# Forming only the first layer's first shift and scale before the first part, and the other modulations at its end

## The reference, cut to what matters

```
mod = (silu(L0_c) @ L0_wmod).reshape(16, 6, 1, 256)   # L0_c 16x256, L0_wmod 256x1536
sa, ca, ga, sb, cb, gb = mod[:, 0..5]
ga = (2 * (ga >= 0) - 1) * maximum(abs(ga), 0.25)     # gb alike
h  = layernorm(x) * (1 + ca) + sa
x  = x + ga * attn0(h, Wq, Wk, Wv, Wlr, Wg, Wo, ...)  # projections, short convolution over 4 taps, SiLU,
                                                      # unit length per head, a recurrence over 32 chunks of 16 tokens
h  = layernorm(x) * (1 + cb) + sb
x  = x + gb * ffn0(h, U1, V1, b1, U2, V2, b2)
# layer 1 the same with L1_c, L1_wmod: windowed attention, then a gated feed-forward part
```

## Time and profile before

| quantity | value |
|---|---|
| median of three runs | 2527.85 us (2524.26 to 2531.57) |
| profiled execution, its own time | 2533.14 us |
| its span | 2531.3 us |
| TensorE (PE) matmul busy | 2166.9 us, 86% |
| VectorE (DVE) busy | 1596.6 us, 63% |
| ScalarE (ACT) busy | 1576.2 us, 62% |
| GpSimd (POOL) busy | 1086.6 us, 43% |
| setup, to the first projection | 0 to 55.5 us |
| part A and its end | 55.5 to 452.4 us |
| mean granted TensorE clock | 0.933 of 2.4 GHz |

### The profile page before, as it was taken

The page is one execution under the profiler, slowest core; times in us unless marked ns, Lnnn a source line. Parts: engine busy times, 40 slices in busy tenths (PEclk is TensorE's granted clock), DMA queues, the critical chain, the costliest instruction groups (busy, mean ns, idle before and its releaser), DMA issues.

```text
span 2531.3 us, 88431 instructions
## 1 busy us (share of the span) xinstructions
PE 2166.9 (86%) x32563; PEld 1390.6 (55%) x32563; DVE 1596.6 (63%) x3896; ACT 1576.2 (62%) x4079; POOL 1086.6 (43%) x1204
## 2 busy tenths in 40 slices
PE   5999997487788787787389999999999999999898
PEld 4554454255555555455246566575664756647466
DVE  1888886477666666667247477474764747647465
ACT  2788787377676666667248466484654846547464
POOL 0122122377677677667524423344233442334323
PEclk8999999699788888889699999999999999999999
DMA  4455555623233233231421231312213122130120
GB/s 150 126 158 164 162 156 160 119 68 85 66 79 74 68 85 76 56 72 39 137 52 31 71 75 43 94 32 66 67 48 94 42 58 60 52 89 4 39 50 18
DMA packets 403135, 201.57 MB, mean 80 GB/s; under 512 B 273776, under 2 KB 389104, under 8 KB 402688
## 3 DMA queue, kind: packets, MB, share of 16 engines
q1 hardware_dynamic: 402688, 195.65, 29.6%
HBM read 101.67 MB, written 69.27 MB: 68 GB/s over the span
## 4 chain that ended last, share of the span: by engine, by line
PE 55%; ACT 15%; issue 12%; DVE 12%; POOL 3%; DMA 1%; SPq 1%; ACTq 0%; DVEq 0%; POOLq 0%
PE psum L982 11%; PE psum L763 6%; ACT arena L1492 6%; ACT arena L1292 5%; PE psum L1075 4%; DVE arena L1785 4%; PE psum L834 3%; PE psum L846 3%; PE psum L1034 3%; PE psum L841 3%; PE psum L1042 3%; PE psum L1111 3%; PE psum L1148 2%; PE psum L1098 2%; PE psum L1129 2%
## 5 line engine op out<-in xcount | busy, mean ns | idle before, releaser
L1716 POOL TENSOR_TENSOR arena<-arena 128x400 f32<-128x400 f32 x256 | 218.3, 853 | 482.8 <-DVE arena L2132 482.8
L1292 ACT ACTIVATE arena<-psum,scan_sb 64x128 f32<-64x128 f32 x1152 | 308.3, 361 | 106.0 <-PE psum L911 88.4
L1492 ACT ACTIVATE arena<-psum,arena 128x100 f32<-128x100 f32 x1024 | 269.5, 365 | 6.0 <-DVE arena L2124 5.9
L1785 DVE SCALAR_TENSOR_TENSOR arena<-psum,taps_sb,arena 128x511 f32<-128x511 f32 (+2 forms) x288 | 213.8, 747 | 60.7 <-ACT arena L1201 53.9
L1534 POOL TENSOR_TENSOR arena<-arena 128x512 f32<-128x512 f32 x64 | 79.4, 1274 | 359.0 <-ACT arena L1227 359.0
L763 PE MATMUL psum<-arena,w_in_sb 128*128 128x512 f32 x512 | 230.0, 598 | 0.9 <-issue 0.9
L841 PE MATMUL psum<-arena 128*32 128x17 f32 x10240 | 134.9, 191 | 98.3 <-issue 65.1
L1852 DVE TENSOR_TENSOR arena<-psum,scan_sb 64x512 f32<-64x512 f32 x290 | 189.0, 673 | 7.6 <-PE psum L942 7.6
L846 PE MATMUL psum<-arena,scan_sb 128*128 128x512 f32 x264 | 186.5, 799 | 1.9 <-DVE arena L1852 1.9
L841 PEld LDWEIGHTS psum<-arena 128*32 128x32 f32 x10240 | 115.5, 117 | 123.1 <-issue 71.7
L2124 DVE TENSOR_REDUCE arena<-psum 128x4 f32<-128x400 f32 x256 | 146.4, 573 | 57.1 <-PE psum L1098 46.7
(11 more groups left out here) (220 smaller groups left out, 4712.2 us busy)
## 6 DMA issues: line engine op xcount, KB each, us to landing
arena<-arena SPq DMA_DIRECT2D x144, 128.0 KB
arena<-x SPq DMA_DIRECT2D x32, 512.0 KB, 3.9
arena<-gates_d SPq DMA_DIRECT2D x112, 128.0 KB, 4.0
v_rows_d<-arena SPq DMA_DIRECT2D x64, 136.0 KB
k_rows_d<-arena SPq DMA_DIRECT2D x64, 136.0 KB
arena<-k_rows_d SPq DMA_DIRECT2D x128, 68.0 KB, 2.0
arena<-v_rows_d SPq DMA_DIRECT2D x128, 68.0 KB, 2.2
v_d<-arena SPq DMA_DIRECT2D x32, 256.0 KB, 4.3
```

The costliest lines, as they stand in the source:

```text
L1292: ins = act.activation(dst.rearrange("p (t x a) -> p t x a", x=PP, a=INNER)[upper, :, x], src.rearrange("p (t a) -> p t a", a=INNER)[upper ...
L1492: act.activation(c_soft[s][:, f % 2, u], sc, ACT.Exp, bias=c_max[s][:, u:u + 1]).then_inc(c_act.mark(f"exp{s}{f}u{u}"), 1)
L1716: pool.tensor_tensor(soft, soft, c_rec[s].unsqueeze(2).broadcast_to([P, 4, KEYS]), ALU.mult).then_inc(c_pool.mark(f"prob{s}{f}"), 1)
L1785: ins = dve.scalar_tensor_tensor(out=a_acc[:, t, j:TOK], in0=bank[2 + t][:, 0:TOK - j], scalar=taps_sb[:, t % KT, col:col + 1], in1=a_acc[ ...
```

## The change

The modulations are now all formed as rows (`mod_row(c)`: 16x512, two of the twelve rows of 256 at once, c = 0 for layer 0's first shift and scale, c = 1 to 5 for the others), and those that are needed as columns are turned afterwards (`mod_turn`, a transpose of a 16x128 piece to 128x16).

Before part A only c = 0 is formed, copied by ScalarE (`row0`), turned with 4 transposes (`mod0`), copied (`modc0`) and its scale raised by 1 (`plus1`). At the end of part A TensorE forms c = 1 to 5 between `turn_v` and `turn_k` of the last sequence, VectorE copies each out of PSUM, forms the gates, copies the 20 turned pieces (`mod1`), adds 1 to the other three scales and makes the bfloat16 identity.

The loads are reordered: `cond`, the first third of layer 0's `wmod` (512 KB), the identity and `parity`, x of sequence 0, `taps`, `w_in`, `mean16`; after x of sequence 1 the rest of `wmod` and the other 22 weights. The waits on all 24 weights become waits on the single ones. `phase_a_done` waits for `identb` and the 22 weights in place of the store of the gates; the last is waited for on SP ahead of the first load of gates in part C.

```diff
-            for layer in range(LAYERS):
-                sp.dma_start(wmod_sb[:, layer], wmod[layer].rearrange("(k p) n -> p k n", p=P)).then_inc(wmod_loaded, 16)
-            for dst, src in ((ident[:], ident_c), (mean16[:], blocks_c), (parity[:], parity_c)):
+            sp.dma_start(wmod_sb[:, 0, :, 0:2 * DIM], wmod[0, :, 0:2 * DIM].rearrange("(k p) n -> p k n", p=P)).then_inc(wmod_first, 16)
+            for dst, src in ((ident[:], ident_c), (parity[:], parity_c)):
                 sp.dma_start(dst, src).then_inc(consts_loaded, 16)
-            for dst, src in (
-                (w_in_sb[:], w_in.rearrange("(k p) n -> p k n", p=P)),
...
-            sp.wait_ge(su_pe.sem, su_pe.before(1, "gate1"))
-            sp.wait_ge(su_dve.sem, su_dve.before(1, "gates"))
-            sp.dma_start(gates_d[0:BATCH], gates_row).then_inc(gates_stored, 16)
...
             load_x(0)
+            sp.dma_start(taps_sb[:], taps.rearrange("(k p) n -> p k n", p=P)).then_inc(taps_loaded, 16)
+            sp.dma_start(w_in_sb[:], w_in.rearrange("(k p) n -> p k n", p=P)).then_inc(w_in_loaded, 16)
+            sp.dma_start(mean16[:], blocks_c).then_inc(blocks_loaded, 16)
             next_x(1)
+            sp.dma_start(wmod_sb[:, 0, :, 2 * DIM:], wmod[0, :, 2 * DIM:].rearrange("(k p) n -> p k n", p=P)).then_inc(wmod_loaded, 16)
+            sp.dma_start(wmod_sb[:, 1], wmod[1].rearrange("(k p) n -> p k n", p=P)).then_inc(wmod_loaded, 16)
+            load_weights()
             next_x(2)
...
+            sp.wait_ge(su_dve.sem, su_dve.at(0, "gates"))
+            sp.dma_start(gates_d[0:BATCH], gates_row).then_inc(gates_stored, 16)
...
+            def mod_row(c):
+                layer, third = THIRDS[c]
+                for k in range(KT):
+                    mm = pe.matmul(bank[max(c + 1, 2)][0:BATCH], cond_silu[:, layer, k], wmod_sb[:, layer, k, third * 2 * DIM:(third + 1) * 2 * DIM],
+                                   start=(k == 0), stop=(k == KT - 1))
+                mm.then_inc(su_pe.mark(f"row{c}"), 1)
...
             pe.wait_ge(su_act.sem, su_act.at(0, "silu"))
+            pe.wait_ge(wmod_first, 16)
+            mod_row(0)
+            pe.wait_ge(consts_loaded, 32)
+            pe.wait_ge(su_act.sem, su_act.at(0, "row0"))
+            mod_turn("mod0", 0, first_rows, 0, 2 * KT)
...
             turn_v(BATCH - 1)
+            pe.wait_ge(wmod_loaded, 16 * LAYERS)
+            pe.wait_ge(pr_act.sem, pr_act.at(BATCH - 1, "g1"))
+            for c in range(1, 6):
+                if c == 3:
+                    pe.wait_ge(le_act.sem, le_act.at(BATCH - 1, "ln3"))
+                mod_row(c)
             turn_k(BATCH - 1)
+            pe.wait_ge(su_dve.sem, su_dve.at(0, "row5"))
+            mod_turn("mod1", 7, other_rows, 2 * KT, LAYERS * N_MOD * KT)
...
-            act.wait_ge(su_dve.sem, su_dve.at(0, "gates"))
+            act.wait_ge(su_dve.sem, su_dve.at(0, "tap"))
+            act.wait_ge(su_dve.sem, su_dve.at(0, "plus1"))
...
+            for c in range(1, 6):
+                dve.wait_ge(su_pe.sem, su_pe.at(0, f"row{c}"))
+                dve.tensor_copy(other_rows[:, (c - 1) * 2 * DIM:c * 2 * DIM], bank[c + 1][0:BATCH]).then_inc(su_dve.mark(f"row{c}"), 1)
+            dve.wait_ge(pr_act.sem, pr_act.at(BATCH - 1, "silu5"))
+            gate_rows_made()
+            dve.wait_ge(su_pe.sem, su_pe.at(0, "mod1"))
+            dve.tensor_copy(modc[:, 2 * KT:].rearrange("p a b -> p (a b)"), bank[7][:, 0:(LAYERS * N_MOD - 2) * KT * BATCH]).then_inc(su_dve.mark("modc1"), 1)
+            dve.wait_ge(su_dve.sem, su_dve.at(0, "modc1"))
+            for j, which in ((2, 4), (3, 7), (4, 10)):
+                add_one(f"plus{j}", which)
+            dve.tensor_copy(identb[:], ident[:]).then_inc(su_dve.mark("identb"), 1)
```

More of the change, by code:

```diff
@@ L140, in adaln_two_layers @@
         cond_silu = carve(LAYERS, KT, BATCH)
[L141 to L144, removed]
+        first_rows = carve(2 * DIM)[0:BATCH]
+        gates_row = carve(2 * LAYERS * DIM)[0:BATCH]
+        THIRDS = [(layer, third) for layer in range(LAYERS) for third in range(N_MOD // 2)]
         top[0] = 0
@@ L711, in _, with mod_turn @@
                 pe.sem_inc(st.sem, len(st.names))
-            pe.wait_ge(wmod_loaded, 16 * LAYERS)
-            pe.wait_ge(su_act.sem, su_act.at(0, "silu"))
[L715 to L728, removed]
+            def mod_row(c):
[4 more added lines that the diff above has]
+                mm.then_inc(su_pe.mark(f"row{c}"), 1)
+            def mod_turn(name, b, rows, first, last):
+                for m in range(first, last):
+                    mm = pe.transpose(bank[b][:, (m - first) * BATCH:(m - first + 1) * BATCH], rows[:, (m - first) * P:(m - first + 1) * P], ident[0:BATCH, 0:BATCH])
+                mm.then_inc(su_pe.mark(name), 1)
+            pe.wait_ge(su_act.sem, su_act.at(0, "silu"))
+            pe.wait_ge(wmod_first, 16)
[3 more added lines that the diff above has]
+            mod_turn("mod0", 0, first_rows, 0, 2 * KT)
             def turn(m):
@@ L752, in project @@
                     elif name in ("q0", "q1"):
[L753 removed]
+                        if behind:
+                            pe.wait_ge(pr_act.sem, pr_act.before(n, ("g0", "g1")[j]))
                     elif behind:
@@ L1169, in _ @@
             act.activation(cond_silu, cond_sb, ACT.Silu).then_inc(su_act.mark("silu"), 1)
[L1170 to L1174, removed]
+            act.wait_ge(su_pe.sem, su_pe.at(0, "row0"))
+            act.activation(first_rows, bank[2][0:BATCH], ACT.Copy).then_inc(su_act.mark("row0"), 1)
+            act.wait_ge(su_pe.sem, su_pe.at(0, "mod0"))
+            act.activation(modc[:, 0:2 * KT].rearrange("p a b -> p (a b)"), bank[0][:, 0:2 * KT * BATCH], ACT.Copy).then_inc(su_act.mark("modc0"), 1)
             def norm_a(m):
@@ L1737, in _ @@
                 dve.sem_inc(st.sem, len(st.names))
[L1738 to L1744, removed]
-            dve.wait_ge(weights_loaded, 16 * 24)
@@ L1752, in _, with add_one @@
[L1752 to L1756 removed]
+            def add_one(name, which):
+                cols = modc[:, which * KT:(which + 1) * KT]
+                dve.tensor_scalar(cols, cols, 1.0, None, ALU.add).then_inc(su_dve.mark(name), 1)
```

105 lines of the change are left out of this document (60 added, 45 removed).

## The result

The changed kernel takes 2552.28 us (median of 4 runs, 2551.34 to 2554.3), the kernel before beside it 2526.06 us (4 runs, 2519.92 to 2531.57). The ratio is 1.009, with a 95% interval of 1.0062 to 1.0118: slower by 26 us (0.9%), where 36.5 us less were forecast, with a range of 2484.5 to 2499. The profiled execution took 2551.96 us, its span 2550.2.

A forecast was written before the change was run, and what follows sets the result against it. Setup before part A was taken as serial, with TensorE idle 9.08 us at part A's end to take the moved work. 37.0 - 0.5 - 0 = 36.5 us off 2527.85 gives 2491.3, range 2484.5 to 2499.

The forecast's parts named there:

- The head: Before part A: first transposes start at 15.7 us where they stood at 52.67, a gain of 37.0, ends 33.9 and 39.
- x of sequence 2: Load in part A, issued half a microsecond late behind the moved weights: 0.5 us of loss counted, ends 0 and 5.
- The end of part A: Five rows fill TensorE's hole before `turn_k` in 8.6 us at the fast clock: no cost, ends 0 and 8.6.
- The rivals on transfers and on slow rows: Early transfers bind: gain 28 to 33.5, chance 0.15; rows slow at part A's end: 7.4 us lost, chance 0.08.
- Part B, the step that failed: Part B's clock wanders from slice to slice, untied to the work; no new mean, noise of 4 us either way.
- turning point: In part B: the change comes out slower once a chunk takes 1.4 us more in the mean.
- part B loses the clock, and the kernel is slower: Rival: engines enter part B from another state; 2 us more a chunk gives 2555; chance 0.03, 0.02 of it ending slower.
- what would show the prediction wrong: First projection after 24 us, row passes at part A's end taking 0.86, or part B over 20 us longer or shorter.

The follow-up runs named there:

- 128 more: The changed kernel with 128 empty semaphore increments added to TensorE's program at the end of part A: 2494.88 us against 2535.31 for the kernel before, ratio 0.9823.
- 64 more: The changed kernel with 64 empty semaphore increments added to TensorE's program at the end of part A: ratio 1.0002 to the kernel before.
- 192 more: The changed kernel with 192 empty semaphore increments added to TensorE's program at the end of part A: ratio 0.9948 to the kernel before.

## Why the prediction was wrong, point by point

- **The head, 37.0 us forecast:** 36.96 came (52.67 - 15.71). The first product started at 5.38 (5.2 forecast), row 0 took 3.57 (3.4, the slow pace), the transposes of the modulations 0.57 (1.0), the copy of 128x64 0.22 (0.3), the first projection stood at 18.61 (18.5).
- **x of sequence 2, a loss of 0.5:** issued at 34.07, it let VectorE start at 41.87, 7.8 us later, where x of sequence 0 alone had taken 3.69 before; so it did stand behind the weights. VectorE had waited 1.96 us for it, and ScalarE took up that layer norm at 43.82, which is no later than the shifted time (81.41 - 36.96 = 44.45). The loss is nothing.
- **The end of part A, no cost:** rows at the fast pace took 8.76 (8.6), `turn_k` waited for POOL, the twenty transposes took 1.41 (2.6 to 5), `identb` was made from 409.30 to 409.52, 5.5 us ahead of SP's 414.98. Right, with more room than was reckoned.
- **The rivals on transfers and on slow rows:** neither came.
- **Part B, the step that failed.** The prediction called the pattern of the granted clock and of the long chunks "not tied to the work" and wrote: "three runs lie within 7.3 us, so the wandering averages out; I see no reason for a new mean". The pattern of the long chunks is tied to the program; it comes back every 8 chunks at the same instructions, with stops at the joints of 16 KB pieces of code. Runs of one program can't show this, since all of them have the same grid; their narrow spread says only that the mean of this program is steady. A change that takes 128 instructions out of TensorE's program ahead of part B gave it another grid and a mean that is 1.66 us a chunk higher (51.5 / 31), a little more than the 1.4 us at which the prediction put the turning point. The rival "part B loses the clock, and the kernel is slower" thus named the right place and turning point, but as a matter of the state in which the engines enter, with a chance of 0.03; its 2555 lies near the measured 2552.28 by luck, since the 2 us a chunk were an example that nothing was worked out from. The lower clock is not shown to be the cause. A part B over 20 us longer was also on the list of what would show the prediction wrong. The cause of the longer part B, as far as the runs show one, is the grid.
- **With the grid put back,** the forecast of the work holds: 128 more gives 0.9823 where 2491.3 / 2527.85 is 0.9855, inside its interval; 34.9 us less by the spans, 36.5 forecast. It beats both kernels, by 40 us that of before (2494.88 against 2535.31).

Left open: how the 51 us divide between the clock and lost overlap; why 64 more is slower in part B than its cuts in `updates` (427, 411, 394, 378, 361 in chunks 3 to 7) would suggest, and by its ratio faster than the changed kernel; the 17 us in part C of 192 more; which remainder is best. The grid is read from the recorded instructions, to within two of them.

## What to carry to other kernels

Before calling a change neutral for the code that follows it, look in the timeline for short groups that are cut in two by "issue", and number the instructions between the cuts: if they lie on a grid of 256, then each instruction added or removed ahead of them moves the grid, and the far stage can lose more than the near one gains. Compare such changes with the remainder held fixed, by filling up with empty instructions to the old number modulo 256, and try two or three fillings once the work is settled. A narrow spread over runs of one program says nothing on whether the next program has the same mean.

## What had not been expected of the hardware

- TensorE stopped 1.0 to 3.2 us at single boundaries of 256 instructions inside groups that it goes through at some 10 ns a recorded product (118 in 1.23 us). Each of the stops over 1.3 us ended 1.2 to 1.8 us behind the end of a packet of its program, in all twelve traces; in longer products (line 846 before, 793 ns each) the idle time from "issue" is nil.
- Behind the jump back of a loop over 8 chunks comes a stop of its own, 1.7 to 3.1 us, where the grid meets the first `scores` behind it.
- An empty increment on TensorE takes 0.153 us: 128 of them lasted 19.6 us (405.97 to 425.60), all but 1.5 us of it inside a wait of 29 us that was there anyway, and 256 lasted 39.2 us and outlasted that wait by 10. In time the 128 thus cost next to nothing, and yet they moved the kernel by -67 us in the one program (0.9823 against 1.009 of 2530) and by +64 us in the other (2599.06 against 2535.31).
